# One TensorE projection moved between the sixth and seventh batch of the recurrence's products

## What is computed

```python
xn = _layernorm(x)
q = silu(causal_dwconv(xn @ Wq.T, qcw, qcb))      # 4 taps, 1024 channels
k = silu(causal_dwconv(xn @ Wk.T, kcw, kcb)) * SCALE
v = silu(causal_dwconv(xn @ Wv.T, vcw, vcb))
a = sigmoid(xn @ Wa.T + ba)
beta = sigmoid(xn @ Wb.T + bb)
def step(S, inp):                                  # scan over the 512 tokens
    qt, kt, vt, at, bt = inp
    err = einsum('bhij,bhj->bhi', S, kt) - vt
    S = at[..., None] * S - bt[..., None, None] * (err[..., None] * kt[:, :, None, :])
    return S, einsum('bhij,bhj->bhi', S, qt)
o = layernorm(o) * ln_w + ln_b, times sigmoid(xn @ Wg.T), then @ Wo.T
```

## Time and profile before

| what | us |
|---|---|
| median of three runs | 7066.73 |
| the profiled execution | 7082.73 |
| its span from first to last instruction | 7080.9 |
| recurrence stage, the 56 looped slots with what stands beside them | 450 to 4070 of the span |
| second stage | from about 4170 to the end |

### The profile page before, as it was taken

One profiled execution on the slowest core, in us unless ns is written; L12 is line 12 of the kernel. 1 busy time (PEld: TensorE's weight loads), 2 busy tenths in 40 slices (PEclk: granted clock), 3 DMA queues, 4 the chain that ended last, 5 costly groups with the idle time before them and its releaser, 6 DMA issues. The chain is left out here.

```text
span 7080.9 us, 176655 instructions
## 1 busy us (share of the span) xinstructions
PE 5011.9 (71%) x58695; PEld 3311.0 (47%) x58695; DVE 5420.1 (77%) x15973; ACT 3320.2 (47%) x7234; POOL 3639.8 (51%) x4232
## 2 busy tenths in 40 slices
PE   5666766666667666667666626888888888888877
PEld 4555555455555555555555523344444444444433
DVE  5889888888898888888888855666666666666665
ACT  4554455445544554455444513444444444444444
POOL 3778777877787778787877761111111111111110
PEclk8877777787777778787777757888888888888888
DMA  4666666666666666666666641111111111111111
GB/s 121 164 159 163 168 164 155 168 167 165 155 168 169 160 158 167 167 167 157 164 168 159 161 123 42 45 45 45 48 45 45 45 45 45 45 45 45 47 45 36
DMA packets 1197390, 804.68 MB, mean 114 GB/s; under 512 B 1049827, under 2 KB 1101699, under 8 KB 1188484
## 3 DMA queue, kind: packets, MB, share of 16 engines
q1 hardware_dynamic: 1134212, 610.21, 36.1%
q10 hardware_dynamic: 62464, 185.09, 8.2%
HBM read 490.57 MB, written 304.55 MB: 112 GB/s over the span
## 5 line engine op out<-in xcount | busy, mean ns | idle before, releaser
L469 POOL TENSOR_TENSOR qp<-qp,ab 128x512 f32<-128x512 f32 (+7 forms) x1024 | 980.0, 957 | 75.3
L474 POOL TENSOR_TENSOR qp<-qp,pt 128x512 f32<-128x512 f32 (+7 forms) x1024 | 961.6, 939 | 80.2
L1778 DVE TENSOR_REDUCE nmax<-w_bank 128x1 f32<-128x512 f32 x1024 | 643.0, 684 | 405.7 <-PE w_bank L1360 401.3
L851 DVE SCALAR_TENSOR_TENSOR p_bank<-y,conv_w,p_bank 128x128 f32<-128x128 f32 x3072 | 825.5, 347 | 50.7 <-ACT p_bank L668 22.8
L1315 POOL TENSOR_TENSOR ot<-ot,ln_w 128x1024 f32<-128x1024 f32 x64 | 150.7, 2355 | 1143.2 <-ACT ot L1617 1143.2
L535 PE MATMUL d_bank<-st 64*32 64x80 f32 x16384 | 493.5, 289 | 340.6 <-issue 315.0
L471 POOL TENSOR_TENSOR pt<-qp,vb 128x512 f32<-128x512 f32 (+7 forms) x1024 | 724.3, 707 | 11.4 <-DVE vb L928 9.3
L507 PE MATMUL d_bank<-xd,kt 32*64 32x128 f32 x7936 | 354.7, 328 | 455.9 <-DVE st L869 392.1
L1320 POOL TENSOR_TENSOR x1b<-x,bias 128x256 f32<-128x256 f32 x64 | 46.3, 723 | 1165.7 <-DVE bst L1874 1165.7
L599 PEld LDWEIGHTS p_bank<-xnT,wqkv 128*128 128x128 f32 x4096 | 548.4, 216 | 187.6 <-issue 187.6
L599 PE MATMUL p_bank<-xnT,wqkv 128*128 128x128 f32 x4096 | 597.1, 306 | 43.1 <-ACT st L681 34.9
(11 more groups left out here) (219 smaller groups left out, 11656.1 us busy)
## 6 DMA issues: line engine op xcount, KB each, us to landing
db<-decay_dram SPq DMA_DIRECT2D x124, 1024.0 KB, 12.3
prod_dram<-prod ACTq DMA_DIRECT2D x128, 640.0 KB, 7.9
kp<-prod_dram SPq DMA_DIRECT2D x512, 80.0 KB, 2.6
qp<-prod_dram SPq DMA_DIRECT2D x256, 160.0 KB, 2.9
a_dram<-at ACTq DMA_DIRECT2D x64, 512.0 KB
ab<-a_dram SPq DMA_DIRECT2D x64, 512.0 KB, 5.8
v_dram<-vt ACTq DMA_DIRECT2D x64, 512.0 KB
vb<-v_dram SPq DMA_DIRECT2D x64, 512.0 KB, 5.7
```

What stands on the lines that cost most here:

```text
L469: link(nc.gpsimd.tensor_tensor(q, q, ab[:, g, r:r + 1, :].to_broadcast([128, w, DV]), ALU.mult), 1)
L474: link(nc.gpsimd.tensor_tensor(q, q, pt2[:, 0:w], ALU.add))
L851: nc.vector.scalar_tensor_tensor(out=zz, in0=y[:, j % Y_BANKS, i, :, tap:tap + C], scalar=conv_w[:, m, tap:tap + 1], in1=zz, op0=ALU.mult, ...
L1778: nc.vector.tensor_reduce(nmax[:, n:n + 1], bank[:], AX.X, ALU.max, negate=True).then_inc(freed, 1)
```

## The change

The eight batches of products are issued by two calls, six batches and then two; between them stands the projection `project(s + 2, g, 2)`, which before stood behind the key transpositions, and the key transpositions now come behind the eighth batch and directly ahead of the scores. The second call repeats the two waits at the head of `products`.

```diff
-            def products(s, n, g):
+            def products(s, n, g, batches):
                 if due(8 * (s - 1)):
                     pe.wait_ge(d_freed, 8 * (s - 1))
                 pe.wait_ge(silu_done, CONV_BANKS * s + 5)
-                for b in range(GB):
+                for b in batches:
...
                     front2(s + 1, n + g, 1 - g, (0, 1))
-                    products(s + 1, n + g, 1 - g)
-                    front2(s + 1, n + g, 1 - g, (2, 3))
+                    products(s + 1, n + g, 1 - g, range(0, GB - 2))
                 if ahead:
                     project(s + 2, g, 2)
                 if front:
+                    products(s + 1, n + g, 1 - g, range(GB - 2, GB))
+                    front2(s + 1, n + g, 1 - g, (2, 3))
                     scores(s + 1, 1 - g)
```

## The result

The changed kernel took 7113.59 us (median of eight runs, 7099.92 to 7122.08) beside 7077.85 us for the kernel before on the same chip (eight runs, 7064.23 to 7097.05). The ratio is 1.0049 with a 95% interval of 1.0033 to 1.0064: 0.0049 x 7078 = 34.7 us slower. Predicted were 34 us. The loss is real, and it lies just inside the half per cent that the prediction took as the border to slower, a border that the interval takes in. The profiled execution of the changed kernel took 7117.07 us, 34.3 more than the one of before; so the two traces may be laid side by side, slot by slot. Their whole times say less about the slots. The last step's `e_dram` is issued at 4218.2 us of the span and not at 4168.3, 49.9 later, so what stands behind it, nearly all of it the second stage that no edit touches, was 15.5 us shorter in this execution.

The account below looks back on a forecast made before the run. The bound was taken as a ring through DVE's solve, `e_dram`, the cross and `xk`; a store 2.6 us later, less slack, costs 0.57 us in 60 slots, 34 us: 7101 us against the median of 7066.73, range 7050 to 7130.

Parts of the forecast that it names:

- the border to slower: Whole kernel: a measurement tells about 0.5%, 35 us, from no change, so slower begins at 7102 us.
- The ring: Slot time: first half of solve, `e_dram`, reading back, `cross`, `x_dram`, `xk`, second half, taps; other work costs only when delaying these.
- The pause and the projection: PE's products: pause keeps its list place, projection falls into low clock; store 2.9 and 2.4 us later, mean 2.6.
- the mean of 1.7: PE's products: lower end of the store's shift, with the projection at the high clock, 2.0 and 1.3 us.
- the sum: SP's list to `e_dram`: shift 2.6 less 0.3 and 0.57 leaves 1.73 us, costing 0.58 a slot, 34 us over 60.
- the rival that had the shift swallowed: Second product store: issued later, it may land sooner in emptier queues; 7 us lost, 7074 us; chance 0.25.
- the two deductions: Taken from the 2.6 us shift: 0.3 us of cover behind `e_dram`, 0.57 us of lost slot time returned as room.
- its own formula: Delay of `e_dram` from shift y, slack spread evenly to 3.9 us: 48/56 x y^2 / 7.8 + 8/56 x y.
- the cover of 0.3 us: Behind `e_dram`: estimated room before PE needs the values read back, since PE waits for them in only 13 slots.
- Late `kp`: DVE's first half: keys exceed 0.8 us of room, losing 45 us in 28 slots, some 12 elsewhere; 7124 us; chance 0.14.
- A higher clock in the cross: PE's second update part and cross: clock 1.0, cross from 3.64 to 2.0 us; about 7048 us; chance 0.11.
- The moved pause: PE's products: pause falls behind the projection, which runs under the code's wait; store unmoved, 7062 to 7067 us; chance 0.08.

Follow-up runs that it names:

- e1: Changed kernel with the projection behind all eight batches and ahead of the key transpositions, so no product waits for it; ratio to the kernel before 1.0007 (0.9996 to 1.0018).
- e10: Changed kernel with the load of `ab` alone issued behind the decay loads, `nb` staying; ratio to the kernel before 1.0014 (1.0004 to 1.0024).
- e11: Kernel before with the load of `ab` alone issued behind the decay loads, control to e10; ratio to the kernel before 0.9995 (0.9984 to 1.0006).
- e5: Kernel before with the loads of `ab` and `nb` both issued behind the decay loads, control to e4; ratio to the kernel before 1.0013 (1.0002 to 1.0023).
- e8: Changed kernel with the load of `nb` alone issued behind the decay loads, `ab` staying; ratio to the kernel before 1.0039 (1.0025 to 1.0053).
- e9: Kernel before with the load of `nb` alone issued behind the decay loads, control to e8; ratio to the kernel before 0.9992 (0.9980 to 1.0004).
- e3: Kernel before with `ab` loaded in four pieces in place of one, PE untouched; ratio to the kernel before 1.0028 (1.0018 to 1.0039).
- e4: Changed kernel with the loads of `ab` and `nb` both issued behind the decay loads; ratio to the kernel before 1.0024 (1.0013 to 1.0036).

## Why the prediction was right, step by step

**What bounds the kernel.** The ring held. The loss is found on it, at PE's wait for `e_dram`, and the new waits on PE and DVE lie under older ones: that of the scores cost nothing that can be told from zero in e1, and DVE's for PE's update parts end ahead of its wait for `xk`, which it still has in all 56 slots. PE's wait for DVE ahead of the updates fell by 1.8 us a slot (353.4 to 252.4 in all), inside the 1 to 2.5 us by which the scores were to end later.

**The pause and the projection.** Right in place and nearly in size. The pause stayed after 166 records and, in the first slot, 5 records into the projection (6 predicted). Behind it came 1.22 + 3.78 + 1.72 = 6.7 us where 6.0 were worked out, and 2.51 + 2.36 = 4.9 where it was 4.7. Counted from the preceding first half, the second store is issued 3.67 us later in the second slots and 3.23 in the first ones; 0.71 and 0.60 of this are the longer slot itself, since the first store is later by as much. That leaves 2.96 and 2.63, where the prediction had 2.9 and 2.4. The Trainium skill, "Runtime: NRT & Kernel Launch", section "Instruction fetch mechanics", has such crossings mostly hidden; the rows of 2042.86 and 2114.75 have 3.17 and 5.23 us of pause in the open, so here too the trace decides. That the pause waits for code is still read from one packet; that it belongs to a place in the list is what the two slots show. One number beside that page was wrong: without any pause the projection would cost 2.0 us in both slots, since the mean of 1.7 counts the pause in the first one.

**From the store to SP's list.** This step failed, in two places. The first: the sum gave SP's next list the lost 0.57 us back as room, since the products hang on the first half. But the first store, too, comes 0.65 us later after the first half (28.94 to 29.59), so the second one stands 3.45 - 0.61 = 2.84 us later against the next first half, and that room is not there. The second goes the other way and is larger, and it is that of the rival that had the shift swallowed: the later store lands sooner after its issue, 4.17 us and not 5.59 in the second slots, 3.49 and not 4.75 in the first ones (means), 1.3 us on average. So the end of the list moved by 1.33 us, from -1.64 to -0.31, where the sum had 2.6 - 0.57 = 2.03. The prediction held against this rival that SP waits for this store in every slot; that shows that a shift is passed on, and not that the store takes as long as before. A likely reason is in the traces: when the second store was issued, the first one had not landed in 50 of 52 slots before, and in 13 of 52 in the changed kernel (16 completions counted; slots 7 to 58). No run tests this by itself.

**From the list to the ring.** With 1.33, and without the two deductions that the sum made from the shift, its own formula gives f = 48/56 x 1.33^2 / 7.8 + 8/56 x 1.33 = 0.38 us; 0.25 was measured, 15 us over 60 slots. The formula itself stands: with `ab` in eight the list moved by 2.98, f = 0.98 + 0.43 = 1.40, and `e_dram` was issued 1.34 later. The deductions do not stand. The room given back was answered above, and the cover of 0.3 us behind `e_dram` was 0.07: of 0.53 us the cross took over 0.46. Both were also made in the expectation for `ab` in eight, which came out too low.

**The term that was missing.** The other 0.28 us of a slot, 17 us over 60 slots, are the slower landing. The prediction took the landing as given, though SP's transfers move with the store, and `ab` with them. 15 and 17 make the 32 us that PE's wait shows. So the number was right by luck: the part that was swallowed and the part that was not seen were of about one size. The chain of the argument was right in its links, but not in the sizes of the shift and of the two deductions, nor in the landing that it took as given.

Here a rule of the Trainium skill would have pointed at it. In "DMA: Bandwidth & Descriptors", section "Queues, rings and completion order", all transfers that SP issues share one ring on each DMA engine, which takes them in order, and a completion is written only after that engine's earlier writes; the page adds that this makes no order of completions between transfers that use different numbers of engines. The slot of 2207.92 agrees: `ab`, `nb`, `decay_dram` and `e_dram` complete in this order at 1.32, 2.93, 3.09 and 3.60 us, and a stall of 1.5 us ahead of `nb` is passed on to `e_dram`. On this reading a transfer on the ring pays for what is still ahead of it in its queue.

**The rivals.** Late `kp`: one wait of 0.7 us, so the 0.8 us of room in the slot shown was not the rule. A higher clock in the cross: it takes 3.64 us at 2020.58 as before, at a granted clock of 0.50. The moved pause: it did not move.

**What stays open.** What stalls the queue for 1.5 us at a time is not shown, and so neither is whether `ab` causes the stalls or only lets them reach `e_dram`; of the 11 slots held up in e10, 6 had nothing of SP's in flight ahead of `e_dram`. The 0.0019 that e10 costs against e11 is not in its `e_dram`: PE's waits for it are 14.8 and 12.4 us. In these two traces more of it stands behind `xk`: from the start of the second half to the end of the next first half it is 37.95 us in e10 and 37.70 in e11 (means of slots 7 to 58). The 0.0013 of e5 has no cause that is shown. e8's trace was taken from one of its quickest executions (7096.92 us, median 7111.63), and at PE's wait for `e_dram` it shows 14 us (31.7, 17.5 in e9) of a loss of 33. e3's loss stands in its trace at `xk`, which lands 0.33 us later although the cross starts 0.11 earlier; but `xk` takes between 7.10 and 7.87 us from issue to landing in the means of the 14 traces, and why is not shown.

## What to carry to other kernels

Work that is put ahead of a store delays all that the store's reader issues behind its wait, however far down the list: follow that list to the first transfer with a reader on the ring, and take its slack from the waits, as a spread and not as a mean. Then look at what is in the queue ahead of that transfer when it is issued: a load of 512 KB that is issued 4 to 5 us ahead of a critical store of half its size went with a later landing here, and moving it behind the critical one (e11) was free. Before a piece of code is inserted, look where the engine pauses without a releaser; here the pauses stayed in their place in the list while the work slid under them, and behind them the granted clock was 0.50.

## What the runs showed of the hardware that was not expected

A store that was issued 2.6 to 3.0 us later landed 1.2 to 1.4 us sooner after its issue, although its bytes are the same; the prediction had allowed for this only as a rival.

The price of issuing a transfer depends on the one ahead of it. `decay_dram` took SP 0.57 us behind `nb` and 2.08 directly behind `ab`; `nb` took 2.28 behind `ab` in one piece and 0.39 behind `ab` in eight. Over the looped slots the means are 0.59 and 1.65, and 1.83 and 0.45. Taking `nb` out of the list therefore gave back less than its row promised. The largest such price was that of whatever came next behind `db` and `ab`: about 12 us, for `nb` in e4 and e5 and for `xt` in e10 and e11.
